# LIF recurrence with k, v, q and output on 32 partitions each and two operations per step

## What is computed

```python
def lif(x_seq, w):
    sg = jax.nn.sigmoid(w)
    def step(v, x):
        h = v + (x - v) * sg
        s = atan_spike(h - V_TH)                  # 1 where h >= 1
        v_new = h * (1.0 - jax.lax.stop_gradient(s))
        return (v_new, s)
    v0 = jnp.zeros_like(x_seq[0])
    _, spikes = jax.lax.scan(step, v0, x_seq)     # over the first axis
    return spikes

xf = x.reshape(T * B, N, C)                       # 128 images of 49 tokens
q = qkv(Wq, wq); k = qkv(Wk, wk); v = qkv(Wv, wv) # lif(xf @ W.T), one step per image
attn = jnp.einsum('tbhnd,tbhmd->tbhnm', q, k) * scale
y = jnp.einsum('tbhnm,tbhmd->tbhnd', attn, v)
y = y.swapaxes(3, 4).reshape(T, B, N, C)
y = lif(y, wa)                                    # over T
out = lif(y.reshape(T * B, N, C) @ Wp.T + bp, wp) # one step per image

x = x + conv(_ln_c(x)); t = tokens(x)
t = t + ffn(_ln_t(t))   # gate softmax, top 2 of 8 experts, gelu(t @ W1 + b1) @ W2 + b2
```

## Time and profile before

| | |
|---|---|
| median of 3 runs | 532.15 us (526.7 to 534.17) |
| profiled execution | 533.05 us |
| its span, first to last instruction | 529.9 us |
| mean granted TensorE clock | 0.776 of full |
| PE, DVE, ACT, POOL busy | 344.2, 384.8, 292.7, 212.3 us |

### The profile page before, as it was taken

The page is one execution under the profiler, slowest core; times in us unless marked ns, Lnnn a source line. Parts: engine busy times, 40 slices in busy tenths (PEclk is TensorE's granted clock), DMA queues, the critical chain, the costliest instruction groups (busy, mean ns, idle before and its releaser), DMA issues.

```text
span 529.9 us, 9576 instructions
## 1 busy us (share of the span) xinstructions
PE 344.2 (65%) x2516; PEld 287.3 (54%) x2516; DVE 384.8 (73%) x1367; ACT 292.7 (55%) x696; POOL 212.3 (40%) x233
## 2 busy tenths in 40 slices
PE   2457654764755756255320499999999999999200
PEld 1133332532532534242220499999999999999200
DVE  4698999989799699978862356666666666665196
ACT  3457674676646757353220266666666666666073
POOL 3000000007265017474777145555555555555400
PEclk9876877566676687555555599999999999999755
DMA  6901000002112012121444222222222222221299
GB/s 168 295 9 25 16 15 17 17 17 61 40 49 57 8 27 66 47 66 46 126 169 117 71 62 74 80 74 78 69 77 71 76 78 72 76 70 44 80 352 308
DMA packets 62148, 43.34 MB, mean 82 GB/s; under 512 B 29057, under 2 KB 56745, under 8 KB 62096
## 3 DMA queue, kind: packets, MB, share of 16 engines
q1 hardware_dynamic: 53648, 28.85, 20.7%
q0 software_dynamic: 6720, 12.97, 7.8%
q10 hardware_dynamic: 1728, 0.94, 0.7%
HBM read 22.09 MB, written 19.91 MB: 79 GB/s over the span
## 4 chain that ended last, share of the span: by engine, by line
PE 48%; DVE 35%; ACT 5%; issue 5%; POOL 3%; DMA 3%; ACTq 1%; POOLq 0%; DVEq 0%; SPq 0%
PE PS L1167 19%; DVE U L892 6%; DVE VV L884 6%; DVE H_all L874 5%; PE PS L1157 5%; PE PS L1159 5%; PE PS L1158 5%; PE PS L1100 3%; PE PS L1037 3%; POOL by_expert L426 3%; DVE stats L642 2%; PE PS L1144 2%; DVE X L1001 2%; PE PS L1028 2%; ACT XG L476 2%
## 5 line engine op out<-in xcount | busy, mean ns | idle before, releaser
L426 POOL DMA_INDIRECT by_expert<-XG,place x98 | 97.4, 994 | 190.3 <-DVE place L796 161.9
L442 POOL DMA_INDIRECT by_token<-osp,target x112 | 110.2, 983 | 94.4 <-issue 79.5
L1167 PE MATMUL PS<-w_now,hid 128*128 128x128 f32 x896 | 108.8, 275 | 0.0
L1167 PEld LDWEIGHTS PS<-w_now,hid 128*128 128x128 f32 x896 | 104.8, 192 | 0.0
L576 ACT ACTIVATE hid<-PS,b1c 128x256 f32<-128x256 f32 x224 | 88.2, 476 | 5.1 <-PE PS L1159 0.7
L582 ACT ACTIVATE w_now<-W_s 128x512 f32 x56 | 35.4, 632 | 69.9 <-PE PS L1167 60.8
L1157 PE MATMUL PS<-rows_high,w_high 128*128 128x256 f32 x224 | 68.4, 305 | 0.4 <-DVE rows_low L960 0.4
L1159 PE MATMUL PS<-rows_high,w_low 128*128 128x256 f32 x224 | 63.7, 284 | 0.0
L1158 PE MATMUL PS<-rows_low,w_high 128*128 128x256 f32 x224 | 63.6, 284 | 0.0
L976 DVE TENSOR_TENSOR osp<-PS,b2b 128x256 f32<-128x256 f32 x56 | 23.7, 424 | 51.1 <-PE PS L1167 51.1
L1037 PE MATMUL PS<-xT,wT 128*128 128x392 f32 x96 | 55.7, 705 | 0.7 <-ACT xT L487 0.7
(11 more groups left out here) (154 smaller groups left out, 576.7 us busy)
## 6 DMA issues: line engine op xcount, KB each, us to landing
rows_in<-by_expert SPq DMA_DIRECT2D x56, 130.0 KB, 2.1
X<-in_x SPq DMA_DIRECT2D x7, 448.0 KB, 6.3
out<-X SPq DMA_DIRECT2D x7, 448.0 KB, 5.7
xT<-by_token SPq DMA_DIRECT2D x3, 896.0 KB, 7.3
H_all<-in_L_ffn_W SPq DMA_DIRECT2D x1, 2048.0 KB, 10.0
by_token<-osp,target POOLq DMA_INDIRECT x112
H_all<-by_token SPq DMA_DIRECT2D x2, 896.0 KB, 11.7
W_s<-by_token SPq DMA_DIRECT2D x2, 896.0 KB, 11.8
```

The source lines that it names most:

```text
L426: pool.indirect_dma_start(by_expert, bass.IndirectOffsetOnAxis(ap=place[g % SENDING][:, k, r:r + 1], axis=0), XG[g % SENDING][:, r, :], No ...
L442: pool.indirect_dma_start(by_token, bass.IndirectOffsetOnAxis(ap=target[b][:, a:a + 1], axis=0), rows_out[b][:, a, :], None, bounds_check= ...
L1167: m = pe.matmul(PS[:, 4 + b % 2, a * 128:a * 128 + 128], hid[b % 2][:, hb, a * 128:a * 128 + 128], w2_now[b % 2][:, hb * C:hb * C + C], st ...
```

## The change

Before, q, k, v and the output stood side by side in columns of H, each on 128 partitions, and their decay factors (they differ between the four) in a tile OM of the same width, so that a step had three operations: H + U, the reset into VV, U = VV * OM. Now k, v, q and the output have 32 partitions each (KP, VP, QP, OP = 0, 32, 64, 96), and a quarter of the channels (j, of GROUPS = 4) stands in a column range. The decay is then one number per partition (part_osg), and a step is two operations: H = VV * part_osg + H, and the reset into VV.

For that the projection weights are arranged so that each of four matmuls gives 96 rows (32 of k, v, q); before, three matmuls gave 128 rows. k and v are transposed in 16 pieces of 64 partitions instead of 8 of 128. q spikes are copied by four DMAs to 128 partitions (q_spikes) for `query`; the output projection is copied by ACT to o_cols and from there by four DMAs to partitions 96 to 127 of H; the output spikes are copied by four DMAs from there to osp. All twelve are on SP's queue. The last LAG blocks of the output have no q, k, v beside them, and have the old form (state VN, reloaded from VV by four DMAs on ACT's queue). LAG is 4 instead of 3, and Y_AT 6 instead of 4. The residual slots are thereby 7, 9, 12, 14, 16 to 20. w2_now shares the memory of KVT.

```diff
-    LAG = 3
+    LAG = 4
+    TAIL = BLOCKS - LAG
+    GROUPS = 4
+    CL = C // GROUPS
+    KP, VP, QP, OP = 0, CL, 2 * CL, 3 * CL
...
-    Y_AT = 4
+    Y_AT = 6
...
-            early += [("qkv", w, slot + 1, 0) for w in range(3)]
-        if 0 <= slot + 1 - LAG < BLOCKS:
-            late.append(("qkv", 3, slot + 1 - LAG, 0))
+            early += [("qkv", j, slot + 1, 0) for j in range(GROUPS)]
+        if 0 <= slot - Y_BEHIND < BLOCKS:
+            late.append(("out", 0, slot - Y_BEHIND, 0))
...
+            def move_q(i):
+                sp.wait_ge(block_done, i + 1)
+                if i >= 2:
+                    sp.wait_ge(y_done, i - 1)
+                for j in range(GROUPS):
+                    sp.dma_start(q_spikes[i % 2][CL * j:CL * j + CL], spikes[i % 2][QP:QP + CL, j]).then_inc(q_in[i % 2], 16)
+            def move_osp(ob):
+                src = spikes[(ob + LAG) % 2]
+                    for j in range(GROUPS):
+                        sp.dma_start(osp[CL * j:CL * j + CL, BC * ob:BC * ob + BC].rearrange("p (s n) -> p s n", n=N),
+                                     src[OP:OP + CL, j, :, 0:N]).then_inc(osp_in[ob % 2], 16)
+            def move_out(ob):
+                sp.wait_ge(ring_copied, item_rank["out", 0, ob, 0] + 1)
+                sp.wait_ge(block_done, ob + LAG - 2)
+                for j in range(GROUPS):
+                    sp.dma_start(H[(ob + LAG) % 3][OP:OP + CL, j].rearrange("p s n -> p (s n)"),
+                                 o_cols[ob % 2][CL * j:CL * j + CL, :]).then_inc(o_in[ob % 2], 16)
...
             for i in range(BLOCKS):
+                move_q(i)
+                if i >= LAG:
+                    move_osp(i - LAG)
+                if 0 <= i - Y_BEHIND < TAIL:
+                    move_out(i - Y_BEHIND)
                 reshape_y(i)
...
                     for st in range(SB):
-                        if slot < BLOCKS:
-                            m = do(v.tensor_tensor(h[:, cur, st, :], U[:, cur, :], h[:, cur, st, :], ALU.add))
...
+                        m = do(v.scalar_tensor_tensor(at(st), state, decay, at(st), ALU.mult, ALU.add))
...
-                        m = do(v.scalar_tensor_tensor(VV[:, cur, :], h[:, cur, st, :], 1.0,
-                                                      h[:, cur, st, :], ALU.is_lt, ALU.mult))
...
+                        m = do(v.scalar_tensor_tensor(state, at(st), 1.0, at(st), ALU.is_lt, ALU.mult))
+                        for point in (3 * st + 1, 3 * st + 2):
...
-                        if slot < BLOCKS:
-                            m = do(v.tensor_tensor(U[:, cur, :], VV[:, cur, :], OM[:, cur, :], ALU.mult))
...
+                        v.tensor_scalar(spikes[slot % 2][0:parts, :, :, 0:N], h[0:parts], 1.0, None,
+                                        ALU.is_ge).then_inc(block_done, 1)
...
-                for w in range(2):
-                    for a in range(4):
-                        k = (w * 4 + a) * 128
-                        m = pe.transpose(bank[:, k:k + 128], pair(1 + w, 4 * i + a), identb[:])
+                for a in range(4):
+                    for j in range(GROUPS):
+                        k = (a * GROUPS + j) * 2 * CL
+                        pair = spikes[i % 2][0:QP, j, 2 * a:2 * a + 2, :].rearrange("p h n -> p (h n)")
+                        m = pe.transpose(bank[:, k:k + 2 * CL], pair, identb[0:QP, 0:QP])
...
             def query(i):
                 pe.wait_ge(kv_masked, i + 1)
+                pe.wait_ge(q_in[i % 2], 16 * GROUPS * (i // 2 + 1))
...
             def turn_out(g):
-                pe.wait_ge(osp_ready, norm2_block(g) + 1)
+                last = min(norm2_block(g), TAIL - 1)
+                for ob in range(max(last - 1, 0), last + 1):
+                    pe.wait_ge(osp_in[ob % 2], 16 * GROUPS * (ob // 2 + 1))
+                if norm2_block(g) >= TAIL:
+                    pe.wait_ge(osp_ready, norm2_block(g) - TAIL + 1)
```

More of the change, by code:

```diff
@@ L270, in metaformer_block @@
         block_done = sem("block_done")
+        q_in = [sem(f"q_in{i}") for i in range(2)]
+        o_in = [sem(f"o_in{i}") for i in range(2)]
+        osp_in = [sem(f"osp_in{i}") for i in range(2)]
+        v_done = sem("v_done")
+        v_in = sem("v_in")
         kvt_turned = sem("kvt_turned")
@@ L489, in copy_item @@
                     return
[L490 to L493, removed]
                 src = bank[:, 0:BC]
-                if w == 3:
+                if kind == "out":
+                    if b >= TAIL:
+                        act.wait_ge(block_done, b + LAG - 2)
+                        dst = H[(b + LAG) % 3][:, 0].rearrange("p s n -> p (s n)")
+                    else:
+                        if b >= 2:
+                            act.wait_ge(o_in[b % 2], 16 * GROUPS * (b // 2))
+                        dst = o_cols[b % 2][:]
                     nc.scalar.activation(dst, src, ACT.Identity, scale=sg[:, 4:5],
                                          bias=bsg[:, 0:1]).then_inc(ring_copied, 1)
-                else:
-                    nc.scalar.activation(dst, src, ACT.Copy, scale=sg[:, w:w + 1]).then_inc(ring_copied, 1)
+                    return
+                if b >= 3:
+                    act.wait_ge(block_done, b - 2)
+                nc.scalar.activation(H[b % 3][0:OP, w].rearrange("p s n -> p (s n)"), src[0:OP], ACT.Copy,
+                                     scale=part_sg[0:OP]).then_inc(ring_copied, 1)
             def copy_kvt(i):
@@ L829, in first_norm @@
                 v.wait_ge(w_in, 16 * 7)
+                for at, col in ((KP, 1), (VP, 2), (QP, 0), (OP, 4)):
+                    do(v.tensor_copy(part_sg[at:at + CL], sg[at:at + CL, col:col + 1]))
+                    do(v.tensor_copy(part_osg[at:at + CL], osg[at:at + CL, col:col + 1]))
+                v.wait_ge(dve, steps.count)
                 v.tensor_tensor(bsg[:], bp_c[:], sg[:, 4:5], ALU.mult).then_inc(sg_ready, 1)
@@ L905, in _ @@
[L905 to L912 removed]
+                            v.wait_ge(kvt_turned, slot - 1)
@@ new lines, in _ @@
+                            v.wait_ge(q_in[slot % 2], 16 * GROUPS * (slot // 2))
+                        if ob >= 2:
+                            v.wait_ge(osp_in[ob % 2], 16 * GROUPS * (ob // 2))
+                        v.tensor_scalar(spikes[slot % 2][0:parts, :, :, 0:N], h[0:parts], 1.0, None,
+                                        ALU.is_ge).then_inc(block_done, 1)
+                    else:
+                        v.tensor_scalar(osp[:, BC * ob:BC * ob + BC], h[:, 0].rearrange("p s n -> p (s n)"), 1.0, None,
+                                        ALU.is_ge).then_inc(osp_ready, 1)
+                        v.wait_ge(osp_ready, ob - TAIL + 1)
+                        v.sem_inc(block_done, 1)
@@ L1044, in ring_item @@
                     m.then_inc(ring_done, 1)
-            def pair(w, p):
-                p *= 2
-                return spikes[p // SB % 2][:, w, p % SB:p % SB + 2, :].rearrange("p h n -> p (h n)")
             def turn_kv(i):
```

109 lines of the change are left out of this document (53 added, 56 removed).

## The result

The kernel after takes **592.26 us** (median of 5 runs, 589.39 to 592.46), the kernel before 532.15: ratio 1.114, 95% interval 1.109 to 1.119. The profiled execution took 589.39 us with a span of 587.7.

What follows compares the result with a forecast made beforehand. Time was set by block 15's end, the way to placing group 4, 48 us of POOL scatters and a fixed rest: block 15 at 263.8 (before 231.0), scatters ending at 341.5 against 293.2, so 533 + 48 = 581, predicted 580; range 548 to 612.

Steps and rivals of the forecast that it cites:

- (1): DVE's recurrence steps: multiplication into U goes, 42 us less over 15 blocks, 5 back for the per-partition factor, net about 37.
- (2): PE and ACT between block end and next input: 16 transposes 1.8 us, fourth projection; first-norm slots 13.3 us, plain near 8.5.
- (3): Slots that choose experts: logits ready 5.9 us after turning starts, 12 us a slot plus 6 or about 1 for late turning.
- the list of signs: What the profile after should show, among it DVE waiting 6 to 12 us at the residual and 2 to 4 for logits.
- (4): Twelve copies on SP's queue: 0.45 us an issue, 5.4 in all, cycle 10.2; SP mostly starts them 3 to 5 late.
- (5): Output spikes at PE's head of slot: landing 2.5 us, PE starts 6.1 to 10.7 late; slots 7, 9, 12, 14 total 97.5.
- Rival (B): Dear copies on SP's queue: issue 0.55 us, landing 4 to 5, SP's cycle 11.4; 600 us, chance 0.16.
- (A): Slower, but cheap copies: SP never late, issues 0.38 us, PE starts on output spikes at 5.2; 555 us, chance 0.2.
- The other eight copies: Copies of q and output's inputs: hidden behind turning, masking and next block; nothing, up to 1 us where SP is 5 late.
- Landing: Arrival of output-spike copies: 2.5 us each; copies inside SBUF not paying for short pieces would give 2.1, y write's row 3.7.
- (6): LAG 4 tail: groups gated one slot later; group 4 placed at 293.5, scatters to 341.5; group 3 would end at 339.5.
- Rival (C): Faster: DVE's work decides, 37 us less, 20 back at residual slots, 3 in the tail; 518 us, chance 0.05.

Runs made afterwards that it cites:

- Experiment 1: Changed kernel without the 48 output-spike copies, PE waiting for the end of the slot alone; leaves out the first 12 blocks' output spikes: 540.35 us, ratio 1.016 to the kernel before.
- experiment 2: Changed kernel with every residual one slot later (norm2_slot + 1), all copies made: 549.51 us, ratio 1.033 to the kernel before.
- experiment 3: Changed kernel with the fourth projection and its ACT copy cut to 8 of 392 columns, leaving out that work: 585.29 us, ratio 1.101 to the kernel before.
- experiment 8: Changed kernel with none of the twelve copies per block (output spikes of the first twelve blocks and output's inputs zero, q's spikes ones): 530.86 us, ratio 1.000.
- experiment 4: Kernel before with LAG = 4 instead of 3 and nothing else: 540.18 us, ratio 1.017 to the kernel before.

## Why the prediction was right

It said 580 us and slower; 592.3 lies 2% above, inside the range. The mechanism is the one it named, the wait for the output spikes at the head of PE's slot (experiments 1 and 2). That the sum came so near is in part luck, since errors of both signs met in it. Its steps:

- **(1) DVE's work.** 1367 to 1246 instructions. Those of the recurrence sum to 132 us instead of 165, 32 less where I had 37; busy time, which counts overlaps once, falls by 26.1. The form with a per-partition factor takes 418 ns, the one with a constant 359, 0.06 apart: the upper bound from the 49-column pair, where I took 0.04.
- **(2) The way through PE and ACT.** Right in kind. The 16 transposes take 1.03 us, as the 8 did, not 1.8. The projection is worth 7 us over the kernel (experiment 3). The reciprocal waits 1.5 us in slots 2 and 4, where I named 2 to 4.
- **(3) Choosing slots.** Predicted 17.4, 17.4, 13.3, 12.4 us for slots 8, 10, 13, 15; by the starts of L957 they took 17.6, 18.7, 13.1, 13.1. I did name the wait "2 to 4" in the list of signs, which is wrong for two of the four (7.60, 8.63, 3.05, 3.35 us); the sum held, since it went by when the logits are ready, not by the wait. It held by luck too: I took 5.9 us from the start of the transposes to the logits, and it was 6.2, 6.6, 5.0 and 5.9, because the transposes took 0.8 us less and the router's products up to 3.6 us instead of 2.2. The 2.2 goes with slot 12 before, where the granted clock at the products was 1.00; in slots 8 and 10 after it was 0.50.
- **(4) and (5) The copies** are where the error is. Issue and lateness were too small, landing too large. An output-spike issue on SP takes 611 ns at the median, the first of the three kinds below:

```profile
L361 SPq DMA_DIRECT2D osp<-spikes x48: 596/611/677, 80.2 to 277.4; - x48
...
DMA to landing us min/median/max: 2.1/2.1/2.7
...
L377 SPq DMA_DIRECT2D y_rows<-y_cols x16: 388/392/587, 38.3 to 286.4; - x16
...
DMA to landing us min/median/max: 3.5/4.2/5.0
```

  The other two kinds have medians of 0.58 and 0.59, so twelve issues are 7.5 us and not 5.4. Where SP never pauses, its cycle from one transposing read to the next is 13.7 us (89.72 to 103.47) and not 10.2: the copies take 8.0 of it with their gaps, and y's write and landing 4.4 instead of 3.7. (The 3.7 of the earlier trace rows mixes the write with the read back; the write alone had 4.0.) SP begins its copies 8.8, 2.9, 5.0 and 3.3 us after the end of the block before slots 7, 9, 12 and 14, where I had 3 to 5, and 0.5 to 1.5 after block 10. In front of slot 7 SP works without a pause; in front of 9 and 14 it waits for y, as forecast; in front of 12 it is 3.7 us late by y and then has a cycle of 13.2 us in a slot of 11.9. PE starts on the output spikes 15.5, 9.6, 11.8 and 9.9 us after the block, against 10.7, 10.2, 6.7 and 9.9 in the sum; what follows takes 13.2 to 14.5 us and not 15, which hides nearly half of the miss. Slots 7, 9, 12, 14 took 29.3, 24.1, 26.0, 23.1, in all 102.5 against 97.5 predicted. Rival (B) had the issue right (0.55) but with a landing of 4 to 5 us, which no row shows; (A) had the landing but not the issue.
- **The other eight copies** I costed at nothing, or up to 1 us. Experiment 1 against 8 puts 9.5 us on them. In slot 6 PE waits 5.5 us, until 94.77, at the head of `query`, which needs q's spikes; SP has issued the last of them by 93.40; the chain that ended last runs through that wait. In slot 7 DVE waits 4.59 us for the output's inputs. There the longer wait behind it covers that one.
- **Landing**: 2.1 us for copies in pieces of 98 bytes, against 4.2 for the y write, also in pieces of 98 bytes, to DRAM. The y write has 1024 pieces and each copy 256, so the nearer comparison is with the output's inputs: the same way, 32 partitions to 32, in pieces of 1568 bytes, 1.9 us. By the rule weighed in the prediction (the Trainium skill, "DMA: Bandwidth & Descriptors", "Why small descriptors are slow (HBM only)") copies inside SBUF don't pay for short pieces; the trace agrees.
- **(6) The tail.** As forecast, the placing of group 4 sets POOL's end, but only just: at 302.45 POOL has waited 0.86 us for it, 0.56 more than its usual 0.30, so that group 3 would have ended 0.6 us earlier and not 2. The last block closes at 272.8 instead of 263.8, and POOL ends at 350.7 instead of 341.5. These 9.0 us are the miss of the profiled execution (589.4 against 581): 3.6 up to block 6, 5.0 in the residual slots, 2.0 in the choosing slots, less 1.6 in slot 11. The median lies 2.9 above that execution.
- **Rival (C)** stood on the residual wait staying under 8 us. Experiment 1 takes that wait away and gets 540 us, experiment 8 all copies and gets 531, not 518: DVE's work didn't decide. (C) had priced the wait for the square root, and not the one for the logits, which took the most.

The mis-sized terms are the issue time on SP, with the lateness that follows from it, and the eight copies costed at nothing.

## What to carry to other kernels

Work taken off the busiest engine of a pipeline is worth only what the other engines' way through the slot leaves: set that way beside the slot's length before and after, and expect the difference as a new wait. When a result that an engine wrote itself now comes by DMA, look for its first reader and what is queued behind that reader: with the same twelve copies the kernel lay 60 us above the one before with the reader at the head of the next slot, and 18 us with it one slot later. And count DMA issues at the time of a row that stands right behind another issue, ahead of whatever the queue's engine does next; on an engine that computes, its next instruction waits for them.

## What the runs showed of the hardware

- On SP's queue a DMA from 32 partitions to 32 others takes 0.58 to 0.61 us to issue (medians). The y write from 128 partitions takes 0.39 to 0.40 after a pause of the queue, but 0.58 to 0.59 the four times that it stands right behind another copy's issue (at 99.06 above, against 120.55), and 0.58 to 0.60 the six times in experiment 2. The kernel before had no other copies in front of it, and its row of 0.38 could not tell the price in a full queue.
- The same 16 router products take 3.58 us in experiment 8 (from 141.69) and 1.95 us in experiment 4 (from 150.92), by the granted clock: 0.50 (the 1.2 GHz level) in the first, 1.00 (2.4 GHz) in the second. Windows of 2 us: PE's busy time, granted clock, DMA share, GB/s; experiment 8 first:

```profile
143.00:145.00 2.00, 2.00 (x11) 0.50 0.20 67
```

```profile
151.00:153.00 2.00, 2.00 (x17) 1.00 0.17 54
```

  In the twelve us before, PE was busy for 9.2 in experiment 8, where the clock stayed low, and for 6.6 in experiment 4, where it rose. With the projections ahead of the products it makes 2.0 us in slot 8 and 2.1 in slot 10, as shown under experiment 8: a part of the wait's growth, and not most of it.
